# Moving the end of a layer norm within a software pipeline: VectorE one step later, ScalarE into the next slot

## What is computed

```python
def _layernorm(x, axis=-1, eps=1e-05):
    m = jnp.mean(x, axis=axis, keepdims=True)
    v = jnp.var(x, axis=axis, keepdims=True)
    return (x - m) / jnp.sqrt(v + eps)

x = L0_attn_hidden_states
x = x + _layernorm(_L0_attn_ref(_layernorm(x, axis=-1), L0_attn_Wq, L0_attn_Wk, L0_attn_Wv, L0_attn_Wo), axis=-1)
x = x + _layernorm(_L0_ffn_ref(_layernorm(x, axis=-1), L0_ffn_A, L0_ffn_B, L0_ffn_Wr, L0_ffn_br), axis=-1)
```

## Time and profile before

| | us |
|---|---|
| median of three executions | 1105.83 (1105.44 to 1107.13) |
| the profiled execution, its own time | 1107.44 |
| its span, first to last instruction | 1105.6 |
| PE busy in the span | 1073.2 (97%) |
| DVE busy | 745.4 (67%) |
| ACT busy | 626.6 (57%) |
| POOL busy | 438.6 (40%) |
| TensorE clock granted in slots 2 to 9 | 1.00 |

### The profile page before, as it was taken

One profiled execution on the slowest core, in us unless ns is written; L12 is line 12 of the kernel. 1 busy time (PEld: TensorE's weight loads), 2 busy tenths in 40 slices (PEclk: granted clock), 3 DMA queues, 4 the chain that ended last, 5 costly groups with the idle time before them and its releaser, 6 DMA issues.

```text
span 1105.6 us, 20082 instructions
## 1 busy us (share of the span) xinstructions
PE 1073.2 (97%) x5556; PEld 886.7 (80%) x5556; DVE 745.4 (67%) x2029; ACT 626.6 (57%) x1437; POOL 438.6 (40%) x413
## 2 busy tenths in 40 slices
PE   7899999999999999999999999999988999999996
PEld 5688787878888888888888888888866888888885
DVE  7677777777666666666666666666665766766676
ACT  6465656566555655555565556555665445455454
POOL 4052524344452625445253543535454233332311
PEclk9999999999999999999999999999998999999999
DMA  6122323231310156021111102112314132323211
GB/s 244 61 80 69 123 66 123 66 124 49 110 49 28 53 181 219 10 72 49 28 53 28 66 9 71 47 29 86 91 48 150 58 113 97 114 87 102 95 58 58
DMA packets 58515, 90.32 MB, mean 82 GB/s; under 512 B 3552, under 2 KB 36320, under 8 KB 58464
## 3 DMA queue, kind: packets, MB, share of 16 engines
q1 hardware_dynamic: 58464, 89.70, 24.8%
HBM read 64.52 MB, written 25.17 MB: 81 GB/s over the span
## 4 chain that ended last, share of the span: by engine, by line
PE 80%; DVE 7%; issue 5%; ACT 5%; DMA 0%; DVEq 0%; POOL 0%; ACTq 0%; POOLq 0%
PE bank L1331 40%; PE bank L1267 29%; PE bank L1358 5%; PE bank L1473 2%; PE bank L1459 1%; PE bank L1309 1%; DVE prob L982 1%; ACT prob L687 1%; DVE q_hl L1014 1%; PE bank L1474 1%; ACT k_hh L713 1%; ACT pT_hi L698 1%; ACT o_low L731 1%; DVE xn L971 1%; DMA xin<-in_x 0%
## 5 line engine op out<-in xcount | busy, mean ns | idle before, releaser
L562 POOL TENSOR_SCALAR prob<-prob,rinv 128x128 f32<-128x128 f32 (+3 forms) x256 | 156.8, 612 | 458.4 <-DVE rinv L992 458.4
L1331 PE MATMUL bank<-big_hi,w_hi 128*128 128x512 f32 x768 | 330.5, 430 | 3.6 <-DVE big_lo L963 3.2
L687 ACT ACTIVATE prob<-prob,nmax 128x128 f32<-128x128 f32 (+3 forms) x256 | 144.0, 562 | 323.1 <-DVE nmax L982 321.9
L1331 PE MATMUL bank<-big_hi,w_lo 128*128 128x512 f32 x768 | 303.3, 395 | 0.0
L1331 PE MATMUL bank<-big_lo,w_hi 128*128 128x512 f32 x768 | 300.8, 392 | 0.0
L1331 PEld LDWEIGHTS bank<-big_hi,w_lo 128*128 128x128 f32 x768 | 144.1, 188 | 33.1
L1331 PEld LDWEIGHTS bank<-big_hi,w_hi 128*128 128x128 f32 x768 | 145.3, 189 | 21.1 <-issue 4.8
L1000 DVE TENSOR_TENSOR pT_lo<-bank,pT_hi 128x128 fp32r<-128x128 f32 (+3 forms) x256 | 123.8, 483 | 54.4 <-ACT pT_hi L698 51.7
L1331 PEld LDWEIGHTS bank<-big_lo,w_hi 128*128 128x128 f32 x768 | 145.8, 190 | 11.3
L982 DVE CUSTOM_DVE_ANT_0 prob<-bank,mask 128x128 f32<-128x128 f32 (+3 forms) x256 | 124.2, 485 | 18.8 <-PE bank L1267 14.5
L992 DVE RECIPROCAL rinv<-rsum 128x1 f32<-128x1 f32 x256 | 40.8, 159 | 134.6 <-ACT prob L687 134.4
(11 more groups left out here) (125 smaller groups left out, 1858.2 us busy)
## 6 DMA issues: line engine op xcount, KB each, us to landing
w_raw<-in_wqkv SPq DMA_DIRECT2D x48, 512.0 KB, 4.2
attention_out<-o_sum SPq DMA_DIRECT2D x64, 128.0 KB, 2.3
xin<-attention_out SPq DMA_DIRECT2D x16, 512.0 KB, 4.7
xres<-in_x SPq DMA_DIRECT2D x16, 512.0 KB, 3.4
out<-res SPq DMA_DIRECT2D x15, 512.0 KB, 2.7
xin<-in_x SPq DMA_DIRECT2D x14, 512.0 KB, 5.3
xT_hold_hi<-xin SPq DMA_DIRECT2D x8, 512.0 KB, 3.6
xT_hold_lo<-xn SPq DMA_DIRECT2D x8, 512.0 KB, 5.4
```

The costliest lines, as they stand in the source:

```text
L562: pool.tensor_scalar(p, p, rinv[:, q % 4:q % 4 + 1], 1.0, ALU.mult, ALU.mult).then_inc(prob_done, 1)
L687: act.activation(prob[:, q % 4, 0:n], prob[:, q % 4, 0:n], ACT.Exp, scale=-1.0, bias=nmax[:, q % 4:q % 4 + 1], accum_out=rsum[:, q % 4:q % ...
L1331: done = pe.matmul(grp_ps[(b + k) % 2][:, :], w, xt, start=at == 0, stop=at == GROUP_MM - 1)
```

## The change

DVE ends the norm (`ln_scale`) in step 7, behind `k_low` and behind the held half, instead of in step 6. ACT writes the normal form in step 1 of the next slot, behind `pt_high`, instead of in step 7. The root's start on ACT (step 6) and the statistics on DVE (step 4) stay.

```diff
                     if b == 1 and s == 4 and not (isinstance(u, int) and u >= UNITS - 1):
                         w_high(0, n + 1)
-                    if prepares(u, ahead) and s == 7:
-                        if ahead:
-                            act.wait_ge(tr_done, fill + 3)
-                        x_normal(ahead_tile(u) + 1)
+                    if ahead and s == 1:
+                        act.wait_ge(tr_done, fill)
+                        x_normal(ahead_tile(u))
...
                     for c in chunks:
                         x_chunk(1, c)
-                    if prepares(u, ahead) and s == 6:
-                        ln_scale(ahead_tile(u) + 1)
                     if ahead and s in HOLD_AT:
                         hold_chunk(u, HOLD_AT.index(s), half, ahead)
+                    if prepares(u, ahead) and s == 7:
+                        ln_scale(ahead_tile(u) + 1)
                     if isinstance(u, int) and STEPS * u + s in WO_DVE_AT:
```

## The result

The changed kernel takes 1111.32 us (median of five, 1110.24 to 1111.89) against 1105.83 for the kernel before: ratio 1.0044, 95% interval 1.0033 to 1.0056. That is a loss of 3.6 to 6.2 us. Forecast were 1110.5 us and a range of 1107.6 to 1112.8. The profiled execution took 1111.89 us with a span of 1110.1, so 4.5 us more than the 1107.44 and 1105.6 before.

The account below looks back on a forecast made before the run. It took a gapless DVE and ACT chain to hold up PE in tile slots 3 to 9. Odd slots 3.4, branch 1.4, others 0, less 0.1 for even slots, gave +4.7 us: 1110.5 us, range 1107.6 to 1112.8.

Parts of the forecast that it names:

- What bounds the tile slots: Slots 3 to 9: PE waits for a DVE and ACT chain without slack; the mask behind the held half decides.
- absorbed: Rival: PE sets the pace, so a later mask costs nothing or only in one or two slots; 1106 to 1107.5, chance 0.13.
- Odd slots: Slots 1, 3, 5, 7: norm on DVE costs 0.84 us each behind the held half, 3.4 us in all.
- gained 0: Odd slots, step 6: taking the norm out gains 0, since ACT's `w_hi` still holds up the exponential.
- The branch: Loop's jump, no longer hidden behind the held half: 0.5 us for slots 3 and 5, 0.2 for 1 and 7; sum 1.4.
- Even slots: Slots 2, 4, 6, 8: norm on DVE gains 0.84 us where removed and fills it again; net 0, less 0.1 in all.
- The sum: Whole kernel: 3.4 + 1.4 + 0 + 0, less 0.1 for even slots, makes +4.7 us.
- The normal form and the load: ACT's form in step 1 fits 1.19 us idle, cost 0, at most 0.1 a slot; SP's load lands 3.2 later, cost 0.
- Load too late: Rival: load lands after 5.9 us, DVE waits about 1.2 us at the statistics of seven slots; 1118 us, chance 0.07.
- Faster: Rival: k's low half ahead of the norm frees PE's wait at the scores, 3.3 us gained; 1102.5 us, chance 0.07.

Follow-up runs that it names:

- the norm in the gap: Kernel before with the norm moved from step 6 to step 7, between mask and reciprocal; 1103.50 us, ratio 0.9973.
- the kernels with one kind of slot: Changed kernel with DVE's part only in even slots: 1106.77 us, ratio 1.0000; only in odd slots: 1111.76 us, ratio 1.0042.

## Why the prediction was right

- **What bounds the tile slots.** At the slot's end, where the change acts, the work of DVE and ACT does. An extra 1.3 us in it made the slot 1.3 us longer; 0.85 less made it 0.85 shorter (the norm in the gap). But the chain of waits isn't theirs alone: in slot 5 before it ran through PE until 155.87, then through DVE and ACT to PE's scores at 175.88. PE isn't far off as a bound: with both waits filled it is busy for all of an odd slot. The rival "absorbed" is out: not even slot 1, ahead of which PE had air, kept its own. Its 1.17 us went through slot 2, which kept to 26.20. PE, which had not waited at v's transposes in slot 2, now waits 0.59 there, and 0.63 instead of 0.36 at those of slot 3.
- **Odd slots.** That the loss lies here is shown by the kernels with one kind of slot, "gained 0" by the norm in the gap. The cost can be read in the rows: from `rr` to the mask are 1.13, 1.34, 1.29 and 0.91 us at the ends of slots 1, 3, 5 and 7, against 0.82 in slot 4. That `w_hi` is the cover is read from ACT's rows and agrees with the kernels that move it, whose exponential starts 0.9 us sooner; a kernel with `w_hi` moved and the norm left in step 6, where the cover should be gone, was not run.
- **The branch.** Taken at 0.5 in slots 3 and 5; measured 0.49 and 0.46 (1.33 and 1.30 less 0.84). Taken at 0.2 in slots 1 and 7; measured 0.33 (1.44 - 0.27 - 0.84) and 0.06. The 0.2 was a guess with no row behind it. Neither slot bore it out, and that their sum did is luck. In slot 1 there is also no held half, so the norm stands behind `k_low`.
- **Even slots.** Taken at 0 less 0.1 for all; measured 0.04, 0.01, 0.03 and 0.17 us less. The last is slot 8, outside the loop: there the norm had cost 1.01 us where it stood (250.73 to 251.74 in the kernel before), not 0.84, and costs 0.80 in its new place (259.38 to 260.18). Together 0.25.
- **The sum.** 1.17 + 1.33 + 1.30 + 0.90 - 0.25 = 4.45 against a forecast of 4.7, and 4.5 between the two spans. The medians differ by 5.5 us. The profile doesn't show the last microsecond of that, and executions of either kernel differ by over 1.5 us.
- **The normal form and the load.** Free, as the kernel with these alone shows. One sign was forecast wrong: ACT's wait for the next mask was to be near 2.2 us, 2.7 at the loop's end, and is 3.44 at the end of slot 7 and 3.83 at the loop's end. The prediction had the form inside ACT's 1.40 us wait. It stood ahead of it, so taking away the form's 1.23 us made the wait longer by about as much. In time it makes no difference. "Load too late" didn't come: 3.3 us to landing and 1.3 to spare (187.63 + 3.3 = 190.9 against 192.22).
- **"Faster".** In even slots its first half came true: PE's wait for k's low half did go. PE then waited longer for v (0.65 instead of 0.38 in slot 5), which hangs on the mask behind the norm, and the slot stayed as long as it was.

What stays open: why the norm takes 0.17 us longer in step 6 of slot 8 than in the loop; what the norm would cost in step 6 of an odd slot without `w_hi` beside it; and how late the load could come before it costs. No run put a price on these.

## What to carry to other kernels

When two engines pass work to and fro without a gap, price a moved instruction at both ends apart: what did it lie beside where it stood, and what will it lie beside where it goes. The same 0.84 us was free behind another engine's longer instruction, free inside a wait for that engine, and paid in full ahead of the instruction that the other engine waits for. Look for a wait in which the instruction fits before moving it "later": here the norm in DVE's wait for the exponential was worth 0.3% of the kernel, and together with `w_hi` in ACT's wait for the next mask 0.6%.

## What the runs showed of the hardware that was not expected

- In this loop the branch was paid when the instruction ahead of it was short and waited for its predecessor: `nmr` to the next mask is 0.75 us with the branch and 0.27 without. With the held half of 0.69 us between them it cost 0.13, and with no norm ahead of the held half nothing (0.60 us to the mask in slot 5 before, 0.61 in slot 4, which has no branch).
- What stands behind the norm decides what the norm costs. The held half started 0.13 us after the start of `nmr` (178.08 to 178.21), the mask 0.27 after it (152.18 to 152.45 in the changed kernel, slot 4). Between `nmr` and the mask DVE's sequencer runs a register operation and a semaphore instruction (L977 and L980, at 152.2 and 152.3); that these are the reason is a reading of the rows and wasn't tested.
- The releaser that the profile named for the mask at the loop's end, PE's transposes, is not in the chain that ends there; the rows of DVE's sequencer are. With the norm ahead of the held half the mask starts at 178.94, while the transposes named (178.64, 0.49 us long) still run.
